# A two-stage preact block on one core: the eight stores of a second-wave row, five and three or four and four

## What is computed

```
x = x + mix(groupnorm(x))        # a 128x128 matrix over positions for each of 4 channel sets, plus a bias
y = groupnorm(x)                 # 32 groups of channels, over all rows and positions of an image
new = y[:, 0]
for h in 1..63:                  # a scan over the rows of an image
    new = y[:, h] + relu(conv1d(new, W))   # 9 taps along the row, 64 to 64 channels
    outs[:, h] = new
return x + outs
```

## Time and profile before

| | |
|---|---|
| median of 3 runs | 750.62 us (749.61 to 754.8) |
| the profiled execution's own time | 750.49 us |
| its span | 748.7 us |
| TensorE busy | 675.1 us (90%) |
| VectorE busy | 588.2 us (79%) |
| ScalarE busy | 505.4 us (68%) |
| GpSimd busy | 438.1 us (59%) |
| stores issued on SyncE, on ScalarE | 832, 192 |
| wave 1's scan | about 510 to 744 us of the span |

### The profile page before, as it was taken

The page is one execution under the profiler, slowest core; times in us unless marked ns, Lnnn a source line. Parts: engine busy times, 40 slices in busy tenths (PEclk is TensorE's granted clock), DMA queues, the critical chain, the costliest instruction groups (busy, mean ns, idle before and its releaser), DMA issues.

```text
span 748.7 us, 18341 instructions
## 1 busy us (share of the span) xinstructions
PE 675.1 (90%) x5044; PEld 640.6 (86%) x5044; DVE 588.2 (79%) x1413; ACT 505.4 (68%) x917; POOL 438.1 (59%) x480
## 2 busy tenths in 40 slices
PE   1588888849999999999999999988999999999995
PEld 1377667738999989999899999988999999999995
DVE  7679999955989788886979798785766777777774
ACT  1188988895687767676676768675666666666661
POOL 1555776614576757565675757834555555555554
PEclk9999999977999999999999999997999999999998
DMA  9956655051555555545554543323444444444444
GB/s 181 172 122 142 145 128 127 16 112 24 105 108 98 90 107 108 103 86 102 107 108 83 105 81 55 53 43 57 72 71 72 75 72 74 73 71 70 70 77 78
DMA packets 412050, 68.18 MB, mean 91 GB/s; under 512 B 411988, under 2 KB 411988, under 8 KB 411988
## 3 DMA queue, kind: packets, MB, share of 16 engines
q1 hardware_dynamic: 359764, 61.17, 44.2%
q10 hardware_dynamic: 52224, 6.30, 5.4%
HBM read 33.85 MB, written 33.55 MB: 90 GB/s over the span
## 4 chain that ended last, share of the span: by engine, by line
PE 49%; DVE 19%; SPq 11%; issue 10%; ACT 6%; DMA 2%; POOL 1%; ACTq 1%; DVEq 1%; POOLq 0%
PE ps_conv L1118 26%; PE ps_conv L1122 13%; SPq L318 10%; PE ps_mix L1009 6%; DVE st L658 5%; DVE x_sb L752 3%; DVE st L766 3%; ACT x_paired L497 3%; PE ps_in L1023 2%; DVE carry L885 2%; DMA x_sb<-in_x_dram 2%; DVE carry_l L895 1%; DVE staged L872 1%; PE ps_small L999 1%; ACT rows L540 1%
## 5 line engine op out<-in xcount | busy, mean ns | idle before, releaser
L416 POOL TENSOR_TENSOR total<-x_paired,carry 128x256 f32<-128x256 f32 (+1 forms) x256 | 238.2, 931 | 222.9 <-DVE staged L872 215.2
L566 ACT ACTIVATE carry_h<-carry 128x256 fp32r<-128x256 f32 x252 | 105.3, 418 | 174.3 <-DVE carry L885 125.6
L1118 PE MATMUL ps_conv<-carry_h,wh 128*128 128x256 f32 x1260 | 202.1, 291 | 5.9 <-ACT carry_h L566 5.9
L540 ACT ACTIVATE rows<-x_paired,shift,rstd 128x256 f32 (+1 forms) x240 | 200.8, 843 | 0.2
L1122 PE MATMUL ps_conv<-carry_l,wh 128*128 128x256 f32 x1260 | 191.3, 282 | 0.8 <-DVE carry_l L895 0.8
L1118 PE MATMUL ps_conv<-carry_h,wl 128*128 128x256 f32 x1260 | 190.7, 282 | 0.0
L895 DVE TENSOR_TENSOR carry_l<-carry,carry_h 128x256 fp32r<-128x256 f32 x252 | 141.4, 561 | 57.7 <-ACT carry_h L566 42.4
L1118 PEld LDWEIGHTS ps_conv<-carry_h,wh 128*128 128x128 f32 x1260 | 168.5, 190 | 11.3 <-ACT carry_h L566 8.8
L1122 PEld LDWEIGHTS ps_conv<-carry_l,wh 128*128 128x128 f32 x1260 | 167.8, 189 | 1.3 <-DVE carry_l L895 1.0
L1118 PEld LDWEIGHTS ps_conv<-carry_h,wl 128*128 128x128 f32 x1260 | 168.3, 189 | 0.0
L380 POOL TENSOR_TENSOR xs<-x_sb,minus_rstd 128x512 f32<-128x512 f32 x104 | 140.3, 1364 | 35.2 <-DVE minus_rstd L734 23.3
(11 more groups left out here) (101 smaller groups left out, 358.6 us busy)
## 6 DMA issues: line engine op xcount, KB each, us to landing
x_sb<-in_x_dram SPq DMA_DIRECT2D x52, 512.0 KB, 4.1
out_dram<-staged SPq DMA_DIRECT2D x832, 32.0 KB, 1.6
rows<-in_x_dram SPq DMA_DIRECT2D x12, 512.0 KB, 4.0
out_dram<-staged ACTq DMA_DIRECT2D x192, 32.0 KB, 1.8
x_paired<-in_L_conv_W_dram SPq DMA_DIRECT2D x2, 80.0 KB, 2.8
x_paired<-in_L_conv_W_dram SPq DMA_DIRECT2D x2, 64.0 KB, 2.5
x_paired<-v_attention_centers_dram SPq DMA_DIRECT2D x1, 0.0 KB
x_paired<-v_attention_spreads_dram SPq DMA_DIRECT2D x1, 0.0 KB
```

The source lines that it names most:

```text
L416: ins = nc.gpsimd.tensor_tensor(summed[:, w0:w0 + n, :], x1_rows(wave, it, i, 1, s * WS + w0, n)[:, 0, :, :], carried[:, w0:w0 + n, :], AL ...
L540: nc.scalar.activation(rows[:, g % 2, :, w // WS, :, w % WS], x1_rows(wave, it, g * RG, RG, w, 1)[:, :, 0, :], ACT.Identity, scale=rstd2[: ...
L566: nc.scalar.activation(carry_h[s][:, EDGE:EDGE + J, :].rearrange("p j w -> p (j w)"), carry[s][:, :], ACT.Copy).then_inc(high_ready[s], 1)
L1118: nc.tensor.matmul(ps_conv[:, s * BANK:s * BANK + SW], w[:, d, :], carry_h[s][:, d:d + J, :].rearrange("p j w -> p (j w)"), start=(w is wh ...
```

## The change

One constant: the number of blocks that SyncE stores in wave 1.

```diff
@@ -53,7 +53,7 @@
 
     x_nat = x.rearrange("b h n c -> n b h c")
     BL = 32
-    SP_BLOCKS = 5
+    SP_BLOCKS = 4
     BLOCKS = 8
     out_blocks = out.rearrange("b h (jh jl q) c -> b h jh jl q c", jl=BL, q=2)
```

## The result

| | before | four and four |
|---|---|---|
| median | 751.35 us (749.61 to 754.8, 4 runs) | 770.33 us (766.11 to 771.41, 4 runs) |
| ratio | | 1.024, 95% interval 1.0206 to 1.0275 |
| the profiled execution | 750.49, span 748.7 | 769.75, span 768.0 |

The change makes the kernel 2.4% slower: 19 us where 12 were forecast, and the cause is the one forecast: one more issue ahead of the half-0 rounding in ScalarE's queue.

The account below looks back on a forecast made before the run. TensorE's 3.54 us a step was taken as the bound by a hair, with a 3.58 two-step chain in the loop. Terms 11.1 + 2.1 - 1.0 = +12.2 gave 763 us, range 756 to 771.

Parts of the forecast that it names:

- the tied chains: In the loop, three loops near 3.81, 3.79 and 3.76 us a step; 2 us added to the upper bound for them.
- The bound before: Wave 1: TensorE's 3.54 us a step bounds by a hair; the loop's chain through ScalarE's issues already takes 3.58.
- Removed from SyncE, nothing: One issue a row fewer on SyncE, which idles over a microsecond a row; worth nothing on the loop's path.
- Added to ScalarE in the loop, +11.1: A fourth issue, 0.463 us, ahead of the half-0 rounding; +0.23 a step over 48 rows, bounds 7.7 to 14.
- the two-step chain: Loop: half-0 convolution through both halves' relu-and-adds, issues and next rounding; 7.16 us per two steps, forecast 7.62, deciding closely.
- the one by VectorE: Loop: half-0 rounding, VectorE's subtraction, half 1's relu-and-add, its rounding, issues; 3.79 us a step, just under 3.81.
- The written-out iterations, +2.1: 13 rows outside the loop: late rounding makes VectorE's subtraction meet GpSimd's addition, 0.16 a step; bounds 0 to 3.0.
- The end, -1.0: Last two rows: SyncE's queue is two issues shorter, so its last store starts about 1.0 us earlier; bounds 0 and -1.4.
- The rule: Skill's rule on issuing engines: only sequencer time is saved, usually small; by it the move is worth about nothing, 750.
- Rival A: At the half-0 rounding: the issuing engine does not matter, only SyncE's relief is left; 748.2 us, chance 0.12.
- B: ScalarE's one-step loop bounds, so all 61 rows pay 0.46 in full; +28, 779 us, chance 0.05.
- C: Half hidden: subtraction escapes GpSimd's addition, half 1 comes 1.77 behind, a one-step loop decides; +6.7, 757 us, chance 0.10.

Follow-up runs that it names:

- e2: Kernel before (five stores a row on SyncE, three on ScalarE) plus a 448-column activation behind ScalarE's three issues in wave 1; ratio 1.0193, 765.91 us.
- e4: Kernel before with six stores a row on SyncE and two on ScalarE instead of five and three; 748.25 us, ratio 0.9943.
- e9: Kernel before (five and three) with GpSimd's half-0 addition in wave 1 cut to one image of four; 751.33 us, ratio 0.9964.
- e1: Changed kernel with block 4 of each wave-1 row not stored, so four on SyncE and three on ScalarE; 751.83 us, ratio 0.9998.
- e7: Changed kernel (four and four) with ScalarE's fourth issue moved directly behind the next step's half-0 rounding; 754.84 us, ratio 1.0035.
- e10: Changed kernel (four and four) with GpSimd's half-0 addition in wave 1 cut to one image of four; 771.68 us, ratio 1.0215.
- e12: Kernel before with three stores a row on SyncE and five on ScalarE instead of five and three; 798.58 us, ratio 1.0592.
- e3: Changed kernel with four and four only in the hardware loop's rows, five and three in the written-out ones; 766.42 us, ratio 1.0201.
- e5: Changed kernel (four and four) with ScalarE's loop written out, so no register work before its issues; 756.85 us, ratio 1.0059.

## Why the prediction was right in kind and short in size

The time, 770.33, lies in the range of 756 to 771, but only just. The bounds of the terms themselves ended at 769; what takes it in is the 2 us added for the tied chains. Those were not meant for a term that was too small, so the range held in part by luck.

**The bound before**: right. That the idle time named after the transposes is queue time is shown by e2 (an activation behind the issues lengthens the step as a fourth issue does), and that the chain stands on the path by a hair by e4 (3.541) and e9 (3.552), whose paces fall to TensorE's.

**Removed from SyncE, nothing**: right: e1, 0.9998, with e7's 0.35% as an upper bound.

**Added to ScalarE in the loop, +11.1**: the mechanism is right, the term was 3.3 too small. Three things are in it.

- An issue was priced at a third of 1.39, 0.463. But the 1.39 of three issues hold two distances and one duration, so the distance is about 0.51, as the starts in the chain of waits above show; four take 1.90 and not 1.85. Both chains move with it: the two-step chain to 7.16 + 0.51 = 7.67, or 3.835 a step, the one by VectorE from 3.79 to 3.84. So the steady step went from 3.58 to 3.84, 48 x 0.26 = 12.5 and not 11.1.
- Which chain decides: I said the two-step one, closely. With the right price the one by VectorE, which closes in one step, is as long: 3.84 against 3.835. e10 shows that it stays when the two-step chain is shortened, e12 that it alone decides from there on. At four issues this cost nothing; for a fifth the forecast's chain would have been out by half.
- The rest, about 2 us, is the two long entries of the loop's first 8 rows (2.86 and 3.08 for 1.90), which no term had. Over the later turns of the loop, 8 rows each, the distance is 31.2, or 3.90; the kernel before has 29.1, or 3.64. 48 times that difference is 12.5, the same as from the steady steps. The upper end of my range had held "stumbles" in it, at 2.9.

**The written-out iterations, +2.1**: 3.3 in the pair, about 2.9 from e3. The mechanism shows as forecast: the rounding comes late, the subtraction meets the addition, half 1's relu-and-add comes 2.10 behind half 0's, and the next half-0 convolution is late. The changed kernel's timeline, the two relu-and-adds and TensorE's first matmuls of half 0:

```profile
519.85 0.42 DVE L885 SCALAR_TENSOR_TENSOR carry<-ps_conv,rows 128x256 f32<-128x256 f32 x1 [0.44 <-PE ps_conv L1122]
...
521.41 0.81 PE L1118 MATMUL ps_conv<-carry_h,wh 128*128 128x256 f32 x5
...
521.95 0.41 DVE L885 SCALAR_TENSOR_TENSOR carry<-ps_conv,rows 128x256 f32<-128x256 f32 x1
...
525.20 0.86 PE L1118 MATMUL ps_conv<-carry_h,wh 128*128 128x256 f32 x5
```

Half 0 starts at 521.41 and 525.20, 3.79 apart, where it was 3.54; the next two steps are 3.67 and 3.79. Over the first four rows ScalarE's issues are 3.86 and 3.59 apart by turns, 3.73 on the average for a forecast 3.70. That e10 takes most of it away confirms the meeting as the cause. The slack of 0.46 was set against an issue of 0.46; the fourth takes 0.50 here too (1.87 for four, 1.37 for three), part of why the term was short.

**The end, -1.0**: -0.35 in the pair. SyncE's queue is shorter as forecast, but of the last five entries on each queue one took over a microsecond. SyncE's and ScalarE's stores from 762.9 us, by line:

```profile
L318 SPq DMA_DIRECT2D out_dram<-staged x5: 316/444/1045, 763.0 to 765.5; - x5
```

```profile
L556 ACTq DMA_DIRECT2D out_dram<-staged x5: 376/472/1103, 763.0 to 765.6; - x5
```

Before, no entry of SyncE's there was over 0.48, and none of ScalarE's. So SyncE's last store starts 2.6 us behind the last transpose where it was 3.0, 0.4 earlier and not 1. In e5, also four and four but without such entries, it is 1.8 behind: the term of 1.0 is about right where they do not fall.

**The start, 0**: +1.9 in the pair, which no term held. I take it as scatter of a part that was not changed.

**The rule** that the issuing engine hardly matters (the Trainium skill, "DMA: Bandwidth & Descriptors", section "Issuing engines are not separate DMA queues") is borne out in what it says: only the sequencer's time differs. It is not small here, though: 0.51 us beside the 1.8 that a store takes to land, and ahead of the rounding in 64 rows it costs 18 to 19 us; the same issue one place later costs 3 (e7).

Rival A is excluded by e2 and by the result, B by the pace (3.95, not 4.1). B's mechanism comes true one issue later (e12). C is excluded in its condition and its time: half 1's relu-and-add is 2.10 behind half 0's and not 1.77, and 770 is not 757. But the chain that it named, the one that closes in one step, is the one left in e10 and e12.

Of the marks that I had named, two fall short of their numbers: ScalarE's entries are x4 but of 1.90 and not 1.85, and their starts are 3.84 apart in the steady steps, as said, but 3.90 over a turn of 8 rows, beyond 3.88. The others hold: an issue on ScalarE did not get cheaper with fewer beside it on SyncE (0.346 recorded in the median, 0.345 before), and transposes did not begin to wait for landings.

## What to carry to other kernels

Issuing a transfer is time in the queue of the engine that issues it. In this profile it stands in no busy share, and the waits show it under the name of something long done. So price it from the distance of two starts, not from a total divided by its count, and ask which instruction stands behind it in that queue. Put issues behind the instruction that another engine waits for, or on a queue that nobody waits for, and stop before that queue's own landings become the wait. Where two chains are near each other, the first unit removed or added may cost half of what the next one costs, so size it on both sides.

## What the runs showed that I had not expected

Single issues that take 1 to 2 us instead of 0.35. They stand at the same places in different kernels: one in the fifth stored row of wave 1 in all but e11 (the three of before take 1.91 there instead of 1.37, the four 2.65 instead of 1.87), and, with four issues at one place on ScalarE, in the first turn of its loop: 2.86 and 3.08 in the changed kernel, 3.68 and 2.18 in e3, 3.54 and 3.35 in e10; with five (e12) 2.95 and 3.76 for 2.40. In the changed kernel's chain the one at 551.68 is the fourth of its row:

```profile
551.68 1.31 ACTq L556
...
553.10 0.42 ACT carry_h L566
```

SyncE's entries stretch in the same moment (four in 2.86 us from 550.13 on), and the store itself lands after 3.0 us instead of 1.8. The kernel before has smaller ones there (1.71 and 1.67 for 1.39), e1 one of 1.66, and e5, whose ScalarE program has no loop, outside the fifth row at most 2.05 for 1.83. Both queues are held up together; what holds them up stays open, none of these runs was made to tell.
